# Normalisation of the residual tiles, order of three context turns, and a split value product in a one-core vision tower kernel

## The reference

```python
h = _L0_tok_ref(x, ...)                                   # (64, 5, 256)
h = concatenate([broadcast(cls_tok), h], axis=1)          # (64, 6, 256)
h = h + _L0_attn_ref(_layernorm(h), Wq, Wk, Wv, Wp, bp)   # causal, 16 heads, ALiBi
h = h + _L0_ffn_ref(_layernorm(h), gate_w, gate_up_w, down_w)
# attention: ctx = softmax(scores) @ v over the tokens j <= i;  out = ctx @ Wp + bp
# ffn: probs = softmax(x @ gate_w); top 2 of 8 experts, weights renormalised
#      expert e: (silu(x @ gate_e) * (x @ up_e)) @ down_e; weighted sum of the two
```

## Time and profile before

| | us |
|---|---|
| median of 3 runs | 213.39 (213.3 to 215.37) |
| the profiled execution | 213.47 |
| its span, first to last instruction | 211.7 |
| PE matmul busy | 194.5 (92% of the span) |
| DVE busy | 140.1 (66%) |
| ACT busy | 108.7 (51%) |
| POOL busy | 80.6 (38%) |

### The profile page before, as it was taken

The page is one execution under the profiler, slowest core; times in us unless marked ns, Lnnn a source line. Parts: engine busy times, 40 slices in busy tenths (PEclk is TensorE's granted clock), DMA queues, the critical chain, the costliest instruction groups (busy, mean ns, idle before and its releaser), DMA issues.

```text
span 211.7 us, 3444 instructions
## 1 busy us (share of the span) xinstructions
PE 194.5 (92%) x1142; PEld 169.7 (80%) x1142; DVE 140.1 (66%) x338; ACT 108.7 (51%) x235; POOL 80.6 (38%) x108
## 2 busy tenths in 40 slices
PE   1999999999999998898967999999999999999991
PEld 1899999998897885876956878988788888888871
DVE  1664976385999998755897448646588677666411
ACT  3575294555327355434831434244487676777320
POOL 4027165274474030366059644485032211122220
PEclk9999999999999999999999999999999999999997
DMA  6999997000491000000004800124999988843003
GB/s 214 339 383 400 303 317 213 3 0 0 138 413 49 0 3 0 0 0 2 3 0 136 362 0 2 37 91 131 374 384 369 326 302 315 301 134 101 0 0 74
DMA packets 10189, 32.90 MB, mean 155 GB/s; under 512 B 1190, under 2 KB 5628, under 8 KB 8508
## 3 DMA queue, kind: packets, MB, share of 16 engines
q1 hardware_dynamic: 8120, 29.53, 39.5%
q10 hardware_dynamic: 1764, 2.37, 3.4%
q0 software_dynamic: 288, 0.79, 1.0%
HBM read 30.05 MB, written 2.64 MB: 154 GB/s over the span
## 4 chain that ended last, share of the span: by engine, by line
PE 66%; DVE 17%; issue 4%; ACT 3%; DMA 3%; POOL 3%; SPq 2%; ACTq 0%; DVEq 0%
PE bank L1053 14%; PE bank L580 10%; PE bank L1071 9%; PE bank L657 6%; PE bank L1084 4%; PE bank L982 3%; DMA raw<-xb 3%; PE bank L992 2%; PE bank L1062 2%; PE bank L604 2%; DVE stats L1678 2%; DVE split L1802 2%; DVE kv_rows L1732 1%; PE bank L722 1%; SPq L468 1%
## 5 line engine op out<-in xcount | busy, mean ns | idle before, releaser
L1053 PE MATMUL bank<-split 128*128 128x512 f32 x132 | 33.2, 400 | 0.5 <-DVE split L2136 0.5
L1611 POOL TENSOR_SCALAR split<-token_row,window 128x384 fp32r<-128x384 f32 x11 | 15.4, 1398 | 46.3 <-PE bank L1084 46.3
L580 PE MATMUL bank<-split 128*128 128x256 f32 (+1 forms) x225 | 28.3, 285 | 0.2 <-DVE split L1804 0.2
L1053 PEld LDWEIGHTS bank<-split 128*128 128x128 f32 x132 | 24.0, 188 | 5.5 <-DVE split L2136 0.7
L580 PEld LDWEIGHTS bank<-split 128*128 128x128 f32 (+1 forms) x225 | 27.5, 191 | 0.5 <-DVE split L1804 0.3
L657 PE MATMUL bank<-split 128*128 128x512 f32 x108 | 26.5, 397 | 0.0
L1515 POOL TENSOR_TENSOR rstd<-veps,mhalf 128x1 f32<-128x1 f32 (+2 forms) x17 | 14.2, 835 | 27.9 <-DVE veps L1685 27.6
L657 PEld LDWEIGHTS bank<-split 128*128 128x128 f32 x108 | 19.8, 188 | 3.9
L1963 DVE TENSOR_TENSOR split<-raw,split 128x512 fp32r<-128x512 f32 x28 | 18.4, 697 | 6.6 <-ACT split L1362 5.2
L1535 POOL TENSOR_TENSOR window<-window,pe_rows 128x256 f32<-128x256 f32 x14 | 14.5, 1034 | 8.6 <-ACT pe_rows L1140 8.0
L1362 ACT CAST split<-raw 128x512 fp32r<-128x512 f32 x28 | 16.5, 620 | 1.9 <-DMA raw<-ffn_w 1.9
(11 more groups left out here) (274 smaller groups left out, 400.4 us busy)
## 6 DMA issues: line engine op xcount, KB each, us to landing
raw<-ffn_w SPq DMA_DIRECT2D x7, 1024.0 KB, 7.5
kv_rows<-ffn_w SPq DMA_DIRECT2D x4, 1024.0 KB, 7.2
raw<-xa SPq DMA_DIRECT2D x5, 768.0 KB
raw<-ffn_w SPq DMA_DIRECT2D x7, 512.0 KB, 8.5
kv_rows<-ffn_w SPq DMA_DIRECT2D x4, 512.0 KB, 6.8
tok<-tok_w SPq DMA_DIRECT2D x1, 1536.0 KB, 12.6
raw<-ffn_w SPq DMA_DIRECT2D x1, 1536.0 KB, 6.4
expert_rows<-zero_row SPq DMA_DIRECT2D x1, 1419.0 KB, 12.9
```

The costliest lines, as they stand in the source:

```text
L580: mm = pe.matmul(bank[b][:, 0:C], xs[0:n, g % 2, px, a:a + P], cws[0:n, pw, k, :], start=(k == 0 and m == 0), stop=(k == len(KCH) - 1 and ...
L1053: mm = pe.matmul(bank[half][:, :], xst[:, s % 2, px, c * P:(c + 1) * P], tile_aws[s % 2][:, piece, pw, :], start=(c == 0 and m == 0), stop ...
L1611: pool.tensor_scalar(back[:, s % 2, :], token_row[:, :], xr[:, s % ROW_RING, ROW_TOKEN:ROW_TOKEN + 1], None, ALU.is_equal).then_inc(back_d ...
```

## The change

- The normalised residual tiles 0 and 1 ("mid0", "mid1") are made by DVE, as tile 2 was; POOL no longer makes their -mean x rstd.
- On DVE all three residual moments and all three normalisations stand ahead of the first `experts_input_lo`.
- PE turns block 1 of the context right behind block 2, ahead of the projection of tile 2; both projections come before the first `turn_mid`.
- POOL makes the first two parts of token 3's value product and DVE the other two (`DVE_VALUES` = 3, also in SP's wait ahead of the second tile's weights).
- ACT copies block 1's context right after block 2's.
- PE turns the rows of slot tile 2 ahead of `tile_out(0)`; DVE's `hidden(1)` stands a few instructions earlier in the picks.

```diff
-NORMED = ["red0", "class", "red1", "in2", "mid2"]
-ACT_NORMED = ["in0", "in1", "mid0", "mid1"]
+NORMED = ["red0", "class", "red1", "in2", "mid0", "mid2", "mid1"]
+ACT_NORMED = ["in0", "in1"]
@@ sp, tile_a
-                    sp.wait_ge(dve_values, 2)
+                    sp.wait_ge(dve_values, DVE_VALUES)
@@ pe
             turn_context(2, 1)
+            pe.wait_ge(pool_values, BLOCKS[0][1] + 2)
+            pe.wait_ge(dve_values, DVE_VALUES)
+            turn_context(1, 4)
             out_proj(2, [(3, "ctx0"), (1, "ctx2")])
-            pe.wait_ge(pool_values, BLOCKS[0][1] + 2)
-            pe.wait_ge(dve_values, 2)
+            out_proj(1, [(4, "ctx1")])
             turn_mid(0, 3)
-            turn_context(1, 4)
             turn_mid(2, 1)
-            out_proj(1, [(4, "ctx1")])
             pe.wait_ge(gate_split, 1)
             wait_free(pe, 2, "router")
             router(0, 3)
@@ pe, slot tiles
-                if GATHERED < s + 1 < SLOT_TILES:
+                if GATHERED <= s + 1 < SLOT_TILES:
                     rows_turn(s + 1)
                 if s:
                     tile_out(s - 1)
                 if s > 1:
                     give_back(s - 2)
-                if s + 1 == GATHERED:
-                    rows_turn(s + 1)
                 hidden_turn(s)
@@ act
             context_copy(2, 1)
-            mid_normalise(0)
+            context_copy(1, 4)
             experts_input_hi(0, 3)
             residual_copy(0)
             token_rows_hi(0)
-            context_copy(1, 4)
             experts_input_hi(2, 1)
             residual_copy(2)
             token_rows_hi(2)
-            mid_normalise(1)
             experts_input_hi(1, 4)
@@ pool
-            values(3)
+            token_values(pool, 3, 0, SHARE).then_inc(pool_values, 1)
             reciprocal_root("mid0", 1)
-            negative_mean("mid0")
...
             reciprocal_root("mid1", 1)
-            negative_mean("mid1")
@@ dve
+            def mid_normalise(j):
+                normalise(f"mid{j}", [bank[ROW_BANK[j]][:, 0:C]], [midn[:, j, :]])
...
             values(4)
+            token_values(dve, 3, SHARE, 4).then_inc(dve_values, 1)
             residual_moments(0)
-            wait_rstd(dve, "mid0")
+            mid_normalise(0)
             tile_weights_lo(0, 0)
             tile_weights_lo(0, 1)
             residual_moments(2)
+            residual_moments(1)
+            mid_normalise(2)
+            mid_normalise(1)
             experts_input_lo(0, 3)
-            normalise("mid2", [bank[ROW_BANK[2]][:, 0:C]], [midn[:, 2, :]])
             experts_input_lo(2, 1)
-            residual_moments(1)
-            wait_rstd(dve, "mid1")
             tile_weights_lo(0, 2)
             tile_weights_lo(0, 3)
             experts_input_lo(1, 4)
@@ dve, picks
             dve.tensor_tensor(slot[:, :, :], counts[:, 0:RT, :], spread(near_first[:, :], 1, RT), ALU.add).then_inc(route_step, 1)
+            hidden(1)
...
             dve.tensor_tensor(slot1[:, :, :], slot[:, :, :], fmask, ALU.mult).then_inc(route_step, 1)
-            hidden(1)
```

More of the change, by code:

```diff
@@ L55 @@
 VSTEPS = 5
+DVE_VALUES = 3
 REST = KCH[-1][1]
@@ L1222, in in_normalise @@
                 normalise(inn[:, j, :], bank[ROW_BANK[j]][:, 0:C], f"in{j}").then_inc(act_normed, 1)
-            def mid_normalise(j):
-                normalise(midn[:, j, :], bank[ROW_BANK[j]][:, 0:C], f"mid{j}").then_inc(act_normed, 1)
             def residual_copy(j):
```

## The result

| | before | changed |
|---|---|---|
| median | 214.0 us (4 runs) | 219.36 us (4 runs, 218.94 to 219.82) |
| ratio | | 1.0243, 95% interval 1.0181 to 1.0305 |
| profiled execution | 213.47 | 219.23 |
| span | 211.7 | 217.4 |

The change makes the kernel slower by 5.4 us in the medians. The forecast was 217.9 with a range to 219.5, so the time lies inside the range, 1.5 us over the point and 0.14 us under its upper end.

The account below looks back on a forecast made before the run. It took the relay for one tile through all engines up to the router as the bound, with PE almost gapless behind; 2.5 (order) + 2.3 (clock) - 0.3 (behind the router) = 4.5 us on 213.39 gave 217.9, range 215.1 to 219.5.

Parts of the forecast that it names:

- Context order and values: Up to the last projection: both projections done at 117.5 instead of 120.0, 2.5 us gained; values' timing hidden by block 2's turn.
- rstd of tile 1 behind `token_rows_lo(2)`: POOL's list: rstd of tile 1 comes at about 121.7, DVE idles about 2.8 us and PE 3.3 us ahead of the routers.
- Routers and `keep_clock(0, 4)` in series: PE ahead of tile 1's turn: filling once hidden now runs in series, so router(1) starts at 127.35, 2.5 us late.
- The clock: PE's gap ahead of router(0): the granted clock falls to 0.50, costing 2.3 us, three quarters of 3.1.
- Behind the router: From router(1) on: two PE waits go, but slot tile 3's weights' transfer lets only 0.3 us through; ends 0 and 0.8.
- The waits of 0.35 and 0.48: PE's waits for hidden(1) and slot tile 2's rows: both removed by the moves behind the router, together 0.83 us.
- one transfer for a gate: Slot tile 3's weights' transfer holds ACT at 153.44 and DVE to 155.79, so PE begins only some 0.3 us sooner.
- The sum: Whole kernel: late order 2.5, clock 2.3, gain behind the router 0.3, together 4.5 us slower.
- the second case: The rival that the clock holds in PE's new gap; chance 0.22, with half taken as 0.12 over 1% slower.
- The clock holds: Rival at PE's new gap: no fall of the clock, 2.2 us slower, 215.6 us (215.0 to 216.3); chance 0.22.
- Faster, rstd isn't late: Rival on POOL: tile 1's rstd comes at 119.3, router(1) no later than before, 212.5 to 213.4 us; chance 0.07.
- The clock stays low longer: Rival from the routers into gate_up: clock low 8 us or more, 4 us lost or more, 219.6 or above; chance 0.08.

Follow-up runs that it names:

- after_rstd_first: The changed kernel with POOL making rstd of tile 1 right behind rstd of tile 2, ahead of second_rows and token_rows_lo of tiles 0 and 2; 215.49 us.
- after_lo_first: The changed kernel with DVE's experts_input_lo of tiles 0 and 2 moved ahead of mid_normalise(1), POOL's list unchanged; 214.44 us.
- after_fill: The changed kernel with keep_clock(0, 6) added on PE ahead of router(0), order of the real work unchanged; 216.10 us.
- after_again: The changed kernel, unchanged, profiled a second time; that execution took 218.49 us.
- before_late: The kernel before with only hidden(1) moved up in the picks and slot tile 2's rows turned ahead of tile_out(0); 212.85 us, ratio 0.9981.
- before_again: The kernel before, unchanged, profiled a second time; that execution took 215.45 us.
- after_no_keep: The changed kernel without keep_clock(0, 4), order of the real work unchanged; 218.18 us.
- lo_first_fill: The kernel after_lo_first with keep_clock(0, 2) added on PE in the gap ahead of the turn of tile 2; 213.02 us.
- before_ctx: The kernel before with only the new context order on PE and ACT's earlier copy of block 1; 214.74 us, ratio 1.0035.

## Why the prediction was right, step by step

- *Context order and values.* I had both projections done 8.6 us after the first turn (117.5 - 108.93); measured 8.4 (119.13 - 110.75). Right. The values were complete 4.0 us after the first turn (DVE's two products end at 114.77) against 4.2 before, and PE's turn of block 2 hid either: the 30 turns run without a gap. Sharing token 3's product gained only that 0.2: POOL's half took 1.26 us where I had 0.85, and DVE's two products 1.58 where I had 1.2, both at work at the same time.
- *rstd of tile 1 behind `token_rows_lo(2)`.* Right in mechanism and size: DVE idle 2.83 us (2.8 predicted), `router(0)` 13.73 us after the first turn (13.8), gap 3.36 (3.3). after_rstd_first shows the cause, after_lo_first that the harm comes through the remainders queued behind.
- *Routers and `keep_clock(0, 4)` in series.* 2.5 us predicted for the order at full clock, 2.2 measured with after_fill.
- *The clock.* It fell, as I expected from the kernel's end. The term was 2.3 us and measured 2.9 (2.8 in after_again): it was under-sized. I took a low stretch of 6.2 us, a quarter of it in the idle gap. It lasted 6.8 us in both profiles, beyond the 4 to 6 that I had named, and of it nothing lay in the gap in the first (it began at 124.9, when PE had work again) and 1.0 us in after_again.
- *Behind the router.* This step was wrong: 0.3 us predicted, 1.2 to 1.3 measured in the first profile of the changed kernel and in before_late. Two errors. The waits of 0.35 and 0.48 are what the timeline shows as idle, but removing them gave 0.57 and 0.73; that the overlap of two records (0.1 to 0.2) is lost with each wait too would fit, but was not tried by itself. And I took one landing time of one transfer for a gate: from issue to ACT's first cast that transfer took 7.1 us before, 6.0 in before_again, 6.2 in the changed kernel and 5.1 in before_late, and slot tile 3 didn't move with it. The wait that does sometimes hold the second move, for the rows read back from memory, I didn't have.
- *The sum.* 2.2 + 2.9 - 1.2 = 3.9 us in the first profile, and 4.4 in after_again (102.16 - 97.79, there the stretch behind the router gained only 0.7). I had 4.5. The medians differ by 5.4, and by 5.4 to 5.7 with the wider medians of the kernel before (213.7 and 213.9 over 24 and 23 runs). So 1.0 to 1.8 us isn't explained by the two profiles of this stage. The dip at the start may be part of it, if it fell unevenly on the runs. And the two slowest runs of the changed kernel (219.49 and 219.82) had a mean granted clock of 0.968 and 0.967, against 0.976 in the profiled one: more time at the lower level, but a mean doesn't say where. That the point came within 1.5 us is partly luck: the clock's term was 0.6 too small and the gain behind the router up to 0.9 too small, with opposite signs.
- *Slips in the working.* Half of the second case's 0.22 is 0.11, not 0.12, and the low end of the range is given as 215.1 in one place and 215.0 in the other. Neither touches the forecast.
- *The rivals.* "The clock holds" would have been near after_fill's 216.1. "Faster, rstd isn't late" describes what the edit of after_rstd_first was meant to turn the kernel into, and not this one; with it the routers come 2.6 us sooner, but the clock fell there too. "The clock stays low longer" (8 us or more, 219.6 or above) is nearer than I gave it: 6.8 us, and the median is only 0.24 under its price. In after_no_keep the low stretch did reach into the dense expert.

## What to carry to other kernels

When work is moved from one engine to another, follow the small instruction that feeds it in the list of its own engine: one rstd of 0.56 us behind four instructions of bookkeeping held two routers for 2.6 us (13.73 against 11.12). Put a waiting instruction behind everything that doesn't need it, not in front. And matmuls that keep the clock are free only in a gap: look whether an edit takes away the wait that hid them.

## What the runs showed of the hardware beyond what I expected

- The clock can fall without a long gap. In after_rstd_first PE's gaps in the 5 us ahead of the fall were 1.35 and 0.73 us, in lo_first_fill 0.49 us in the 4 us ahead of it, and in both the granted clock went to 0.50 while PE was at work. It also fell in before_ctx, at 120.2, after gaps of 1.37 and 0.35 us. PE's work ahead of these falls was turns of 128 columns, projections and fillers of 256, and routers of 8; which of it matters was not tried. In the kernel before, with `keep_clock` at the same place and gaps up to 1.08 us, the clock held in both profiles, and so it did in after_lo_first with a gap of 1.33.
- How long it stays low differs as much: 3.4 us in after_rstd_first, 6.8 in both profiles of the changed kernel, where `keep_clock` followed the routers, and 10.2 in after_no_keep, where it didn't.
- One wait for data at 13 to 15 us makes the same program take 1.5 us more or less over 45 matmuls (7.16 or 5.65), depending on whether the clock falls behind it. It fell after waits of 1.59 (the changed kernel), 1.87 (after_rstd_first) and 1.96 us (before_again), and held after one of 1.27 (after_lo_first). Comparing two profiles of two kernels without measuring from a common point would have put 1.8 us on the change.
- The same transfer of weights, issued behind the same work, took 5.1 to 7.1 us from issue to first use, and 7.1 and 6.0 us in two executions of one program. A landing time read from one profile is one draw, not a gate.
